# Moving a gather from behind the wait for a scattering addition to ahead of it, in a kernel of graph layers and experts

## The chip, the cores and the metric

One core of one Trainium2 chip runs the whole program. The metric is device microseconds of one execution; the time before is the median of three timed runs. The core has five engines with their own instruction streams: TensorE (PE), VectorE (DVE), ScalarE (ACT), GpSimd (POOL) and SyncE (SP). They meet at semaphores only. DMAs are issued from POOL's, SP's and ACT's streams and run on 16 DMA engines; each adds 16 to a semaphore when it has landed.

## The reference

3125 nodes with 256 features go through four blocks, each added to its input: a graph network of three layers with batch norm, an attention over 64 slices, a second graph convolution of two layers, and a mixture of experts. Only the last one is touched:

```
logits = xt @ Wr + br;  probs = softmax(logits)
top_p, top_idx = top_k(probs, 2);  weights = top_p / top_p.sum()
xn = (xt - mean) * rsqrt(var + 1e-5)
xe = xn * ln_g[e] + ln_b[e]                      # for each of 8 experts
h  = gelu(xe @ W1[e] + b1[e])                    # 256 -> 1024
y  = h @ W2[e] + b2[e]                           # 1024 -> 256
out = x + sum over the two chosen experts of weight * y
```

## The kernel before

The graph blocks come first and end at about 2550 us. Then the router picks two experts for each node. The kernel computes only chosen pairs of node and expert: it sorts them by expert into units of 128 rows, and units into 32 chunks (CHUNKS) of one expert each. Each chunk has two units, but every fourth has one (UNITS_OF, L53): a turn (TURN = 4) has 2, 2, 2 and 1 units, 56 in all. The loops of the engines run over eight turns g of four chunks j; chunk c = 4g + j uses buffer s = c % 2 of everything that is double: the gathered rows xin, the expert's weights w1e and w2e, the outputs yrow, the banks of PSUM.

One chunk c passes through these steps, named by their lines:

- POOL gathers its rows from the DRAM table xn_rows into xin[c % 2], one indirect DMA for each unit (gather_rows, L616 to L621). Its index table, from_row, comes from the router (r_dve reaches 3). Before the buffer is written again, TensorE must have read chunk c - 2 from it: e_tps counts the transposed chunks.
- SP loads W1 of the chunk's expert and its vectors (load_rows, L483 to L488) when ScalarE is done with chunk c - 2, and W2 and b2 (load_second, L490 to L493) when VectorE is done with the outputs of chunk c - 2 (e_y).
- TensorE turns the rows (turn_rows, L2069), waiting for row_in, the gather's semaphore; VectorE applies the expert's norm vectors (L1615); TensorE computes the hidden layer (hidden, L2079: 32 matmuls), ScalarE its GELU (L902), and TensorE the outputs (outputs, L2088: 16 matmuls for each unit, as 32 instructions in the profile for two).
- VectorE adds b2 (L1623) and multiplies by the gate (L1625) into yrow[c % 2], and adds one to e_y. It waits for y_used at c + 1, that is, until the additions of chunk c - 2 have landed.
- POOL adds the rows to x_sum in DRAM, one indirect DMA with addition for each unit (L642). A node can stand in two chunks, and two additions to one row must not be in flight together, so POOL waits for all of a chunk's additions to land (y_added, L644) before it issues those of the next; then it adds one to y_used (L645).

TensorE's order is fixed: transposes of chunk c + 1, outputs of chunk c, hidden layer of chunk c + 1 (turn_of_chunks, L2095 to L2104). POOL's order is the loop at L635 to L645. Before the loop POOL gathers chunks 0 and 1 (L631, L632) and waits until x_sum is stored (moe_stored) and the index table of the additions is there (r_dve reaches 4). In the loop, iteration c first gathers chunk c + 2 and then adds chunk c. After the last chunk SP and ACT wait for y_used and copy x_sum to the output.

Of the kernel before, what the change touches and what calls it, by code (L numbers as in the profile page):

```python
# [43 lines left out]
CHUNKS = PAIRS + SINGLES  # L44
# [51 lines left out]
def build(nc, x, src, dst, w, out):  # L96
    ctx = ExitStack()
    with ctx:
# [219 lines left out]
        def fresh(tag, *names):  # L318
            return [sem(f"{tag}_{n}") for n in names]
# [25 lines left out]
        e_tps, e_xe, e_hps, e_gelu, e_yps, e_b, e_y = fresh("expert", "transposed", "inputs", "hidden", "gelus", "outputs", "biased", "rows_out")  # L345
# [168 lines left out]
        def _(pool):  # L514
# [101 lines left out]
            def gather_rows(c):  # L616

                for i in range(UNITS_OF[c]):
                    j = UNIT_AT[c] + i
                    nc.gpsimd.indirect_dma_start(out=xin[c % 2][:, i, :], out_offset=None, in_=xn_rows,  # L620
                                                 in_offset=bass.IndirectOffsetOnAxis(ap=from_row[:, j:j + 1], axis=0)).then_inc(row_in[c % 2], 16)  # L621
# [8 lines left out]
            pool.wait_ge(r_dve, 3)  # L630
            gather_rows(0)  # L631
            gather_rows(1)  # L632
            pool.wait_ge(moe_stored, 16 * 5)
            pool.wait_ge(r_dve, 4)
            for c in range(CHUNKS):  # L635
                if c + 2 < CHUNKS:
                    pool.wait_ge(e_tps, c + 1)
                    gather_rows(c + 2)
                pool.wait_ge(e_y, c + 3)
                for i in range(UNITS_OF[c]):  # L640
                    j = UNIT_AT[c] + i
                    nc.gpsimd.indirect_dma_start(out=x_sum, out_offset=bass.IndirectOffsetOnAxis(ap=to_row[:, j:j + 1], axis=0),  # L642
                                                 in_=yrow[c % 2][:, i, :], in_offset=None, compute_op=ALU.add).then_inc(y_added, 16)
                pool.wait_ge(y_added, 16 * sum(UNITS_OF[:c + 1]))  # L644
                pool.sem_inc(y_used, 1)  # L645

# [2 lines left out]
        def _(act):  # L649
# [195 lines left out]
            def conv_rows(k):  # L845

                _, tps, tcp, xps, hi, _ = conv

                def copy(t, i):
                    wait(tps, t + (k * T + BT + 1))  # L850
                    nc.scalar.activation(feat[:, 0:2, i * P:(i + 1) * P], ps[:, i % 2, 0:F].rearrange("p (f c) -> p f c", f=2), ACT.Copy).then_inc(tcp, 1)

                def high(t, i):
                    wait(xps, t + (k * T + 1))
                    nc.scalar.activation(conv_halves[0][0][:, bass.ds(t, 1), 0:F], ps[:, 2 + i % 2, 0:F].unsqueeze(1), ACT.Copy, scale=sc[:, 0:1]).then_inc(hi, 1)

                if k == 0:
                    block_sqrt(0)
                    wait(sc_ready, 3)
                    for t in range(T + 1):  # L860
                        if t < T:
                            copy(t, t % BT)
                        if t >= 1:
                            high(t - 1, (t - 1) % BT)
                        if t % BT == 2 and t // BT + 1 < NB:
                            block_sqrt(t // BT + 1)
                else:
                    wait(sc_ready, 4)
                    three_stages(act.Fori(1, NB), copy, high, nothing)
# [772 lines left out]
        def _(pe):  # L1642
# [54 lines left out]
            def enter_block(l, b, tile_rows, weights, last=HB):  # L1697

                rows, _, lo = ent[l][0:3]
                for h, tiles in ((0, (0, 1)), (1, (2, 3, 4))):  # L1700
                    for i in tiles:
                        pe.wait_ge(lo, b * BT + (2 if i == 4 else 1))
                        for f in range(4):
                            if i == tiles[0]:
                                pe.wait_ge(rows, b * 8 + (4 * h + f + 1))
                            ins = tile_rows(i, f)
                        ins.then_inc(ent[l][3], 1)
                    half_products(l, b, h, weights, HB if h == 0 else last)
# [253 lines left out]
            def conv_rows(k):  # L1962

                rows, tps, tcp, xps, _, lo = conv

                def turn(t, i):
# [166 lines left out]
```

## Time and profile before

| | |
|---|---|
| timed runs | 3054.23 us median (3053.55 to 3055.42, three runs) |
| the profiled execution's own time | 3055.43 us |
| its span, first to last instruction | 3053.6 us |
| mean granted TensorE clock | 0.868 of full speed |
| TensorE busy | 2275.3 us, 75% of the span |
| POOL busy | 888.4 us, 29%, of which the gathers and additions of the expert chunks are a small part |
| first gather of the stage, last addition issued | 2592.7 us, 3037.1 us |

The profile is one execution, recorded by the hardware. Line numbers (L620) are those of the kernel's code. A row of the timeline gives start, busy time, engine, line, operation, what is written and read, how many instructions are merged, and in brackets how long the engine was idle before and who ended that. harena and ring are large buffers in SBUF in which xin, xeT, yrow and the experts' weights lie under their own names: in this stage a POOL row that writes harena from xn_rows is a gather, and ring is W1 and W2. "issue" is time in which nothing that the profile shows was waited for.

### The profile page before, as it was taken

The numbers are of one execution on the slowest core, as the hardware profiler recorded it, in microseconds if no ns is written. First come the engines' busy times: TensorE is split into PE (matmuls) and PEld (weight loads), VectorE is DVE, ScalarE is ACT, GpSimd is POOL, SyncE is SP. The second block draws the span as 40 slices with busy tenths as digits, with TensorE's granted clock in tenths as the row PEclk, the third lists the DMA queues.
The fourth block names the chain that finished last, engine by engine and source line by source line (L and its number), as shares of the span: only waits on it lengthen the run. The fifth ranks groups of instructions, "written<-read, shape, count | busy, mean of one in ns | idle before, by whom it ended". The sixth has DMA issues, their size and how long they took to land.

```text
span 3053.6 us, 39654 instructions
## 1 busy us (share of the span) xinstructions
PE 2275.3 (75%) x14187; PEld 1775.8 (58%) x14187; DVE 1314.2 (43%) x2799; ACT 375.8 (12%) x789; POOL 888.4 (29%) x638
## 2 busy tenths in 40 slices
PE   1033100069779999999988977999899995999997
PEld 1022100046557776778763456888688884788886
DVE  7899999954431111111127743113311667111111
ACT  0011000000015000004002202000210000222221
POOL 4888888878800000000011300000100001233332
PEclk6566555579989999999998969999999996999998
DMA  9943333398550999950460000444234434566665
GB/s 338 339 67 48 42 55 48 35 310 249 137 192 0 181 260 218 261 172 0 137 192 0 0 1 11 150 145 148 83 119 150 138 103 128 162 194 208 185 191 170
DMA packets 287137, 425.19 MB, mean 139 GB/s; under 512 B 165698, under 2 KB 222553, under 8 KB 286975
## 3 DMA queue, kind: packets, MB, share of 16 engines
q1 hardware_dynamic: 104895, 295.72, 29.9%
q10 hardware_dynamic: 109760, 108.33, 13.1%
q0 software_dynamic: 72400, 20.04, 7.8%
q8 instruction: 51, 0.84, 0.1%
q14 instruction: 31, 0.25, 0.0%
HBM read 306.57 MB, written 100.17 MB: 133 GB/s over the span
## 4 chain that ended last, share of the span: by engine, by line
PE 59%; POOL 16%; DVE 10%; issue 7%; DMA 5%; ACT 2%; DVEq 0%; ACTq 0%; SPq 0%; POOLq 0%
PE ps L1762 16%; PE ps L2008 8%; PE ps L2009 8%; POOL at_counts L552 8%; POOL odd_counts L552 7%; PE ps L2088 6%; PE ps L1780 4%; PE ps L1694 4%; PE ps L2079 4%; DMA x_sum<-harena 2%; PE ps L1951 2%; PE ps L1848 2%; DMA xrows<-odd_counts 1%; PE ps L1977 1%; DMA harena<-xn_rows,harena 1%
## 5 line engine op out<-in xcount | busy, mean ns | idle before, releaser
L2008 PE MATMUL ps<-harena,ring 128*128 128x257 f16 x2500 | 556.7, 275 | 3.7 <-DVE harena L1361 2.7
L2009 PE MATMUL ps<-harena,ring 128*128 128x256 f16 x2500 | 556.4, 274 | 0.0
L1762 PE MATMUL ps<-ring,harena 128*128 128x320 f16 (+1 forms) x4000 | 539.2, 297 | 1.4 <-ACT tarena L713 0.8
L1762 PEld LDWEIGHTS ps<-ring,harena 128*128 128x128 f16 x4000 | 391.9, 98 | 144.6 <-issue 3.1
L1056 DVE SCALAR_TENSOR_TENSOR late<-ring,ps 128x1024 f16<-128x1024 f32 x312 | 378.9, 1275 | 12.3 <-DMA ring<-key_rows 10.1
L552 POOL DMA_INDIRECT at_counts<-harena x208 | 330.7, 1590 | 110.0 <-issue 104.0
L552 POOL DMA_INDIRECT odd_counts<-harena x208 | 328.7, 1580 | 63.7 <-issue 61.8
L2008 PEld LDWEIGHTS ps<-harena,ring 128*128 128x128 f16 x2500 | 243.7, 97 | 43.2 <-DVE harena L1427 3.8
L2009 PEld LDWEIGHTS ps<-harena,ring 128*128 128x128 f16 x2500 | 243.2, 97 | 33.0
L1786 PE MATMUL ps<-ident,sc 128*1 128x128 f32 x8 | 2.1, 365 | 288.5 <-DVE sc L1004 288.5
L2088 PE MATMUL ps<-ring,harena 128*128 128x256 f32 x896 | 202.2, 384 | 7.8 <-ACT harena L902 6.6
L2079 PE MATMUL ps<-harena,ring 128*128 128x256 f32 (+1 forms) x1024 | 202.5, 357 | 1.2 <-DVE harena L1615 1.2
L2079 PEld LDWEIGHTS ps<-harena,ring 128*128 128x128 f32 x1024 | 178.0, 193 | 22.2 <-issue 1.6
L2088 PEld LDWEIGHTS ps<-ring,harena 128*128 128x128 f32 x896 | 169.0, 191 | 34.9 <-issue 13.5
L1137 DVE SCALAR_TENSOR_TENSOR feat<-ps,sc,late 128x640 f32<-128x640 f32 x30 | 26.5, 883 | 348.5 <-PE ps L1762 348.5
L577 POOL DMA_DIRECT2D wl<-L_ffn_W_out x1 | 0.7, 712 | 586.8 <-DVE feat L1137 586.8
L1786 PEld LDWEIGHTS ps<-ident,sc 128*1 128x1 f32 x8 | 0.4, 81 | 290.2 <-issue 284.0
L902 ACT ACTIVATE harena<-ps,harena 128x256 f32<-128x256 f32 (+1 forms) x256 | 114.4, 447 | 358.6 <-PE ps L2079 354.2
L1371 DVE TENSOR_SCALAR late<-ps 128x1 f32<-128x1 f32 x100 | 15.4, 154 | 325.0 <-PE ps L2009 325.0
L1780 PE MATMUL ps<-feat,wl 128*128 128x320 f32 x480 | 134.8, 442 | 18.3 <-DVE feat L1137 17.2
L609 POOL COPY feat<-tarena 128x256 f32 x25 | 9.8, 400 | 438.0 <-DVE tarena L1432 414.3
L642 POOL DMA_INDIRECT x_sum<-harena x56 | 89.1, 1590 | 145.1 <-DVE harena L1625 135.7
(382 smaller groups left out, 2620.1 us busy)
## 6 DMA issues: line engine op xcount, KB each, us to landing
ring<-at_counts SPq DMA_DIRECT2D x150, 800.0 KB, 4.5
ring<-L_ffn_W SPq DMA_DIRECT2D x64, 1024.0 KB, 5.5
ring<-ad_counts SPq DMA_DIRECT2D x50, 800.0 KB, 4.2
ring<-key_rows SPq DMA_DIRECT2D x52, 512.0 KB, 3.8
at_counts<-tarena ACTq DMA_DIRECT2D x5, 4000.0 KB, 15.0
odd_counts<-tarena ACTq DMA_DIRECT2D x5, 4000.0 KB, 27.2
xrows<-odd_counts SPq DMA_DIRECT2D x25, 800.0 KB, 8.3
at_counts<-ring ACTq DMA_DIRECT2D x25, 800.0 KB, 7.5
```

The costliest lines, as they stand in the source:

```text
L552: nc.gpsimd.indirect_dma_start(out=table, out_offset=bass.IndirectOffsetOnAxis(ap=eidx[:, c:c + 1], axis=0), in_=evalue[:, c:c + 1], in_of ...
L642: nc.gpsimd.indirect_dma_start(out=x_sum, out_offset=bass.IndirectOffsetOnAxis(ap=to_row[:, j:j + 1], axis=0), in_=yrow[c % 2][:, i, :], i ...
L902: nc.scalar.activation(hT[s][:, k, 0:n], ps[:, k % 4, 0:n], ACT.Gelu, bias=evc[s][:, k:k + 1]).then_inc(e_gelu, 1)
L1056: ins = V.scalar_tensor_tensor(out=ejunk[q], in0=krow[:, s, :], scalar=ekey[:, bass.ds(g + q, 1)], in1=weight_ps[:, GE - P - q * P:2 * GE ...
L1694: ins = M(ps[:, 4 + n % 4, 0:c], weights[:, d, fo * P:(fo + 1) * P], feat[:, d, h * HB:h * HB + c], start=(d == 0), stop=(d == 3))
L1762: ins = M(ps[:, 2 * f + h, 0:c], part[:, t, (2 * k + f) * P:(2 * k + f + 1) * P], chunk[q][:, s, h * HB:h * HB + c], start=(t == 0 and par ...
L1780: ins = M(ps[:, k + h, 0:HB], wl2[:, d, fo * P:(fo + 1) * P], feat[:, d, h * HB:(h + 1) * HB], start=(d == 0), stop=(d == nfi - 1))
L1848: return M(ps[:, i % 4, 0:F], feat[:, d, i * P:(i + 1) * P], wl3[:, d, :], start=(d == 0), stop=(d == 3))
L2008: M(ps[:, i, 0:F + 1], lhs, hh[:, t, 0:F + 1], start=(t == 0), stop=False)
L2009: ins = M(ps[:, i, 0:F], lhs, hl[:, t, :], start=False, stop=(t == T - 1))
L2079: ins = M(ps[:, k % 4, 0:n * P], w1e[s][:, d, k * P:(k + 1) * P], xeT[s][:, d, 0:n * P], start=(d == 0), stop=(d == 1))
L2088: ins = M(ps[:, 4 + s, i * F:(i + 1) * F], hT[s][:, k, i * P:(i + 1) * P], w2e[s][:, k, :], start=(k == 0), stop=(k == EK - 1))
```

## The change

POOL's loop gathers three chunks ahead instead of two, and at another place: after the additions of chunk c are issued and before the wait for their landing. Chunk 2 is gathered ahead of the loop. A gather of chunk c + 3 writes buffer (c + 3) % 2 = (c + 1) % 2, so it waits for the transposes of chunk c + 1 (e_tps at c + 2). All other engines' streams are the same.

```diff
             gather_rows(0)
             gather_rows(1)
+            pool.wait_ge(e_tps, 1)
+            gather_rows(2)
             pool.wait_ge(moe_stored, 16 * 5)
             pool.wait_ge(r_dve, 4)
             for c in range(CHUNKS):
-                if c + 2 < CHUNKS:
-                    pool.wait_ge(e_tps, c + 1)
-                    gather_rows(c + 2)
                 pool.wait_ge(e_y, c + 3)
                 for i in range(UNITS_OF[c]):
                     j = UNIT_AT[c] + i
                     nc.gpsimd.indirect_dma_start(out=x_sum, out_offset=bass.IndirectOffsetOnAxis(ap=to_row[:, j:j + 1], axis=0),
                                                  in_=yrow[c % 2][:, i, :], in_offset=None, compute_op=ALU.add).then_inc(y_added, 16)
+                if c + 3 < CHUNKS:
+                    pool.wait_ge(e_tps, c + 2)
+                    gather_rows(c + 3)
                 pool.wait_ge(y_added, 16 * sum(UNITS_OF[:c + 1]))
                 pool.sem_inc(y_used, 1)
```

## Rows read from the trace of the kernel before

**Rows 1.** The page, part 4: the chain that ended last, by line.

```profile
PE ps L1762 16%; PE ps L2008 8%; PE ps L2009 8%; POOL at_counts L552 8%; POOL odd_counts L552 7%; PE ps L2088 6%; PE ps L1780 4%; PE ps L1694 4%; PE ps L2079 4%; DMA x_sum<-harena 2%; PE ps L1951 2%; PE ps L1848 2%; DMA xrows<-odd_counts 1%; PE ps L1977 1%; DMA harena<-xn_rows,harena 1%
```

**Rows 2.** Waits, 2590 to 3053 us: who for whom, total us, times, longest.

```profile
DVE harena L1623 <- PE ps L2088: 180.9, 32, 7.0
...
POOL harena L620 <- DMA x_sum<-harena: 130.5, 25, 7.8
...
PE ps L2069 <- DMA harena<-xn_rows,harena: 21.8, 8, 5.1
```

**Rows 3.** Timeline of PE: a boundary without a wait, two with one.

```profile
2616.79 7.07 PE L2079 MATMUL ps<-harena,ring 128*128 128x256 f32 x32
2623.70 0.60 PE L2069 MATMUL ps<-ident,harena 128*128 128x128 f32 x4
2624.56 7.17 PE L2088 MATMUL ps<-ring,harena 128*128 128x256 f32 x32 [0.26 <-ACT harena L902]
...
2654.23 7.07 PE L2079 MATMUL ps<-harena,ring 128*128 128x256 f32 x32
2663.80 0.66 PE L2069 MATMUL ps<-ident,harena 128*128 128x128 f32 x4 [2.50 <-DMA harena<-xn_rows,harena]
2664.29 7.07 PE L2088 MATMUL ps<-ring,harena 128*128 128x256 f32 x32
...
2708.63 7.07 PE L2079 MATMUL ps<-harena,ring 128*128 128x256 f32 x32
```

**Rows 4.** The chain in order of time: start us, us, what.

```profile
2650.28 8.55 DMA x_sum<-harena
...
2660.99 2.77 DMA harena<-xn_rows,harena
...
2704.68 6.27 DMA x_sum<-harena
...
2713.11 5.25 DMA harena<-xn_rows,harena
...
2923.61 8.25 DMA x_sum<-harena
```

**Rows 5.** Timeline of POOL: gathers (L620), additions (L642).

```profile
2598.75 0.94 POOL L620 DMA_INDIRECT harena<-xn_rows,harena  x1 [1.15 <-PE ps L2069]
...
2650.28 1.59 POOL L642 DMA_INDIRECT x_sum<-harena  x1 [0.31 <-issue]
2659.67 1.01 POOL L620 DMA_INDIRECT harena<-xn_rows,harena  x1 [7.81 <-DMA x_sum<-harena]
```

**Rows 6.** Landings: additions L642; gathers L620; the gather issued at 2711.8.

```profile
DMA to landing us min/median/max: 3.7/6.4/8.6
...
DMA to landing us min/median/max: 2.7/3.5/5.2
...
DMA to landing us min/median/max: 4.7/4.7/4.7
```

**Rows 7.** Two us: engines' busy time; last PEclk, DMA share, GB/s.

```profile
2656.00:2658.00 2.00, 2.00 (x11) 1.77 (x10) 0.00 (x0) 1.00 (x3) 0.00 (x0) 1.00 1.07 345
```

**Rows 8.** W1 issued at 2651.4, its landing; all W2 (L492); VectorE's timeline.

```profile
L486 SPq DMA_DIRECT2D ring<-L_ffn_W x1: 378/378/378, 2651.4 to 2651.4; - x1
...
DMA to landing us min/median/max: 7.9/7.9/7.9
...
DMA to landing us min/median/max: 5.2/5.6/10.4
...
2671.49 0.69 DVE L1623 TENSOR_TENSOR harena<-ps,harena 128x512 f32<-128x512 f32 x1 [5.90 <-PE ps L2088]
```

**Rows 9.** PE's timeline in turn 4, and five us of it (last PEclk, DMA share, GB/s).

```profile
2826.89 1.12 PE L2069 MATMUL ps<-ident,harena 128*128 128x128 f32 x4 [2.31 <-DMA harena<-xn_rows,harena]
2827.80 8.22 PE L2088 MATMUL ps<-ring,harena 128*128 128x256 f32 x32
...
2825.00:2830.00 5.00, 3.11 (x10) 2.67 (x11) 0.99 (x2) 0.14 (x1) 1.50 (x2) 0.67 0.79 219
```

## The prediction

> **What bounds the kernel now.** I read the page's chain first [rows 1]: matmul lines fill it; the additions into x_sum landing are 2% of the chain, the gathers landing 1%. The change lies in the last stage alone, the 32 expert chunks from 2592 us on, so everything ahead of it stays. The second view, the waits of that stage [rows 2], says who is late there. TensorE's transposes (L2069) wait for gathered rows 8 times, 21.8 us together. VectorE's L1623 waits for TensorE in all of its 32 turns, never for additions to land. POOL waits 130.5 us for landings: long, and costly only where it holds back a gather that TensorE wants.
>
> The third view, TensorE's own order of time, says where [rows 3]. At a boundary without a wait (2616.79) the transposes come 6.91 us behind the start of the hidden layer L2079, and the outputs L2088 7.77 us behind it. The boundary at 2654.23 has the same instructions, but 2.50 us of idle before the transposes. It is the same place in each turn of four chunks (of two, two, two and one unit): the transposes of chunk 4g+5. There are seven, g = 0 to 6. The eighth wait is the first gather of the stage, 5.10 us from 2591.7 to 2596.83, which the change leaves alone. So the seven make 21.8 - 5.1 = 16.7 us.
>
> The chain of that stretch and POOL's order show why there [rows 4, 5]. The second addition of chunk 2 is issued at 2650.28 and lands after 8.55 us, at 2658.8; POOL wakes, issues the gathers of chunk 5 at 2659.67 and 2660.99, and the latter lands 2.77 us on, at 2663.8. TensorE could have used the rows from 2654.23 + 6.91 = 2661.14. Chunk 3 has one unit and so half the matmuls of the others: this interval is some 7 us shorter (half of 7.07 + 7.17) [rows 3] than those that hide the same sequence.
>
> **The change, part by part.** Nothing is added or removed: 56 gathers and 56 additions before and after, the same waits on the same semaphores. Three things move.
>
> The gather of chunk 2 moves ahead of two waits, for stores and for indices. It still waits for the first transposes, and its issue at 2598.75 came 1.15 us behind its forerunner and right behind them [rows 5], so the two waits cost nothing there: 0 us.
>
> The gathers of chunk c+3 move from behind the landing of chunk c's additions to ahead of it. For chunk 5, POOL issues them at 2650.28 + 1.59 + 0.30 = 2652.2 and, 1.01 and 0.30 later, at 2653.5: 7.5 us earlier than before. Their own wait, for chunk c+1's transposes, never holds: TensorE runs those before outputs(c), and outputs(c) comes before the additions. How long do they take to land? Gathers of the stage take 2.7 to 5.2 us, median 3.5 [rows 6]; the long one was issued at 2713.11 [rows 4] into full DMA engines, and they are as full here (share 1.07 in 2656 to 2658) [rows 7]. So I take the upper end: 2653.5 + 5.2 = 2658.7, 2.4 us before TensorE wants them, and the stall goes whole. With 2.7 us they land at 2656.2, which brings no more. No gather of this trace was issued with an addition still in flight ahead of it; that bound is under rival A.
>
> The step "landed, count up" (y_used) moves past two gathers, 2 x 1.3 = 2.6 us of POOL. The shortest landing is 3.7 us [rows 6], 1.6 of it the issue itself, so the step is late by 0.5 us at most. VectorE asks for it at L1623 two chunks on: for chunk 2's additions, landed at 2658.8, at 2671.49 [rows 8]. Some 12 us of cover, 10 after the change: 0 us. POOL's next additions come earlier, as the gathers no longer stand before them.
>
> SP's queue is not passed, only its DMA engines shared: two units (128 rows of 256 fp32 each, 0.26 MB) now travel while the weights do, of which W1 alone has 1 MB. W1 of chunk 5, issued at 2651.4, lands in 7.9 us, at 2659.3, and is wanted by the next hidden layer, at 2669 after the change; W2 of chunk 4, issued with chunk 2's additions, is wanted at 2661.9, over 13 us on, and the longest landing of any W2 is 10.4 us [rows 8]. A quarter megabyte against the load that took 7.9 us is 2 us at most, less than either cover (9.7 and 3.3): 0 us. What is late next at the boundary is ScalarE's last GELU, 0.26 us as at 2624.56 [rows 3].
>
> **The sum.** L2079 to L2088 takes 2664.29 - 2654.23 = 10.06 us with the stall and 7.77 without: 2.29 us. The outputs behind a stall are busy 7.07 us, elsewhere 7.17 [rows 3], so 0.1 goes back. That is 2.2 us for 2.5 us of idle: 0.3 less, because transposes that come late hide behind nothing. Over seven, 16.7 - 7 x 0.3 = 14.6 us. Turn 4 has more: after 2.31 us of idle the granted clock was 0.67 in 2825 to 2830 (of the levels 2.4 and 1.2 GHz, the lower for two thirds of that time), the transposes took 1.12 instead of 0.66 us and the outputs 8.22 instead of 7.07 [rows 9]. That is 1.6 us, which goes too if the idle was what let the clock fall; six equal stalls did not make it fall, so it may not be in each execution. Against the profiled one (span 3053.6, time 3055.43): 16.2 us, so 3039.2. The median of the runs, 3054.23, lies 1.2 below that one, about this clock event; less 14.6 it gives 3039.6. I predict 3039.5.
>
> **A rule beside the rows.** The row: chunk 2's second addition lands 8.55 us after its issue, at 2658.8 [rows 4]. The Trainium skill's "DMA: Bandwidth & Descriptors" says, in "Queues, rings and completion order", that a DMA engine takes the descriptors of one ring in order, and that a semaphore's increment lands only after every earlier write of that engine, whatever the queue. By that rule the gathers, in POOL's queue behind the additions, cannot be counted in before 2658.8, however early they are issued. No row of this trace has a gather behind an addition in flight.
>
> **Rivals.**
> *A. The gathers queue behind the additions.* They then land one unit at a time after the last addition. Under load the two gathers of turn 2 landed 1.9 us apart (2711.80 + 4.7 and 2713.11 + 5.25) [rows 4, 6]; at best both come in with the addition. So 0 to 3.8 us after it. From addition to need there are 2661.14 - 2658.83 = 2.3 us in turn 1, and 2715.54 - 2710.95 = 4.6 in turn 2; three turns have additions like the first (8.55 to 8.25 us) [rows 4]. These three keep 0 to 1.5 us of wait each, 0 to 4.5 us in all; with 2.5 us, 3042.0. For it: one queue. Against it: the additions' 8 us may be a wait for the weights' loads that the gathers share and need not repeat.
>
> *B. The stall is DMA volume, not order.* TensorE restarts 9.57 us after L2079's start in turn 1 and 9.77 in turn 2 (2718.4), although the additions took 8.55 and 6.27 us; the gathers made up for it with 2.77 and 5.25 [rows 3, 4]. That looks like rows that come in when the weights' backlog clears, whatever POOL does. If they then land at 2662.8 instead of 2663.8, the gain is 7 x 1 us: 3047. Against it: W1 of chunk 5, four times the two units and issued 2 us ahead of their new place, was in at 2659.3 [rows 8].
>
> *C. Slower: gathers and additions in one queue hold each other up.* The additions read and write x_sum in DRAM, the gathers read beside them. If a gather issued at 2653.5 takes over 10.3 us (to 2663.8, where TensorE starts today), each boundary is later than now; at 12 us, 1.7 x 7 = 12 us more, 3066. It decides from twice the longest gather of the trace. For it only that the pair is never seen in flight together; against it that two additions together still land in 8.6 us.
>
> *D. Order isn't what holds the gathers.* If POOL could not issue a gather before the additions ahead of it are done, the time stays at 3054. Against it: the second addition is issued 0.31 us behind the first [rows 5], with that in flight.
>
> **Chances.** Forecast (stall gone, 3037 to 3041) 0.60; A 0.23; B 0.09; C 0.04; D 0.04. The range, 3036.5 to 3046.5, holds the forecast with and without the clock event, A to its worst bound and part of B. A measurement here tells about 0.2% (6.1 us) from no change. Faster by more: forecast, A and two thirds of B, 0.89. Within: the rest of B, and D, 0.07. Slower: C, 0.04.
>
> **What would show it.** In the changed kernel's waits of the stage, L2069 should have one wait for gathered rows (5.1 us) and at most a few under 1 us; L2079 to L2088 7.8 us in all turns; a turn of 52 us, not 54.4 (2654.23 to 2708.63). POOL's gathers stand 0.3 us behind additions. The landing of the boundary gathers tells the forecast from A: 3 to 5.2 us, or behind the addition each time. B shows as landings at the same distance from L2079 as now, C as landings above 10 us. I am wrong if TensorE gets a new wait, on weights or on y_used by way of VectorE, or if those gathers take over 7.6 us.

## The result, and the profile after

The changed kernel takes 3039.19 us (median of five runs, 3039.01 to 3042.78), the one before 3055.42 (3053.55 to 3065.41). The ratio is 0.9945, 95% interval 0.9925 to 0.9964: faster by 0.55%, well clear of 0.2%. The forecast was 3039.5; the five runs after the change alone spread over 3.8 us, so part of that closeness is luck. The profiled executions have spans of 3037.4 and 3053.6 us, 16.2 apart, which is the sum that the prediction made against the profiled execution.

Two lines stand above the loop now, so other lines have shifted: L2071 are the transposes (L2069 before), L2081 the hidden layer (L2079), L2090 the outputs (L2088), L1625 VectorE's first step on them (L1623), L641 the additions (L642); the gathers stay L620.

The waits of the expert stage, who for whom, total us, times, longest:

```profile
POOL x_sum L641 <- DVE harena L1627: 233.9, 25, 17.9
DVE harena L1625 <- PE ps L2090: 183.3, 32, 6.9
...
POOL x_sum L641 <- DMA x_sum<-harena: 25.7, 7, 5.4
...
PE ps L2071 <- DMA harena<-xn_rows,harena: 5.3, 1, 5.3
```

Of the eight waits for gathered rows one is left, the first of the stage; before it was 21.8 us in eight [rows 2]. VectorE still waits for TensorE alone, 32 times. POOL waits for landings only seven times, ahead of the additions of the one-unit chunks; the rest of its time it now waits for outputs, as it should.

TensorE's order of time, at a boundary that had no wait and at two that had one:

```profile
2616.97 7.07 PE L2081 MATMUL ps<-harena,ring 128*128 128x256 f32 x32
2623.88 0.60 PE L2071 MATMUL ps<-ident,harena 128*128 128x128 f32 x4
2624.74 7.17 PE L2090 MATMUL ps<-ring,harena 128*128 128x256 f32 x32 [0.26 <-ACT harena L904]
...
2654.41 7.07 PE L2081 MATMUL ps<-harena,ring 128*128 128x256 f32 x32
2661.32 0.60 PE L2071 MATMUL ps<-ident,harena 128*128 128x128 f32 x4
2662.18 7.17 PE L2090 MATMUL ps<-ring,harena 128*128 128x256 f32 x32 [0.27 <-ACT harena L904]
...
2706.62 7.07 PE L2081 MATMUL ps<-harena,ring 128*128 128x256 f32 x32
```

L2081 to L2090 is 7.77 us at both, where it was 10.06 at the second [rows 3]; a turn is 2706.62 - 2654.41 = 52.21 us, where it was 54.40. The granted clock shows it too, in five us of turn 4 (the last three numbers are granted clock, DMA share, GB/s): 1.00 with TensorE at work, where 2825 to 2830 had 0.67 [rows 9].

```profile
2815.00:2820.00 5.00, 4.73 (x25) 3.96 (x24) 0.99 (x2) 2.13 (x5) 2.74 (x3) 1.00 1.04 303
```

POOL's order at the boundary, and two landings, of the addition issued at 2650.45 and of the gather issued at 2653.67:

```profile
2650.45 1.59 POOL L641 DMA_INDIRECT x_sum<-harena  x1 [0.30 <-issue]
2652.35 1.01 POOL L620 DMA_INDIRECT harena<-xn_rows,harena  x1 [0.30 <-issue]
2653.67 0.99 POOL L620 DMA_INDIRECT harena<-xn_rows,harena  x1 [0.30 <-issue]
2657.19 1.61 POOL L641 DMA_INDIRECT x_sum<-harena  x1 [2.53 <-DMA x_sum<-harena]
```

```profile
DMA to landing us min/median/max: 5.9/5.9/5.9
...
DMA to landing us min/median/max: 6.2/6.2/6.2
```

The gather takes 6.2 us, not 2.77 as before or 5.2 as forecast, and lands at 2659.87, 3.5 us behind the addition and 1.45 us ahead of the transposes. The seven boundaries, in us from the issue of the second addition (before: landing of the addition, then TensorE's restart on the rows; after: the same landing, the second gather's landing and TensorE's transposes, which did not wait):

| turn | before: addition, restart | after: addition, gather, transposes |
|---|---|---|
| 1 | 8.55, 13.52 | 5.9, 9.4, 10.87 |
| 2 | 6.27, 13.72 | 6.4, 9.2, 10.86 |
| 3 | 6.70, 13.38 | 7.0, 9.5, 10.85 |
| 4 | 6.25, 13.33 | 8.7, 9.7, 10.85 |
| 5 | 8.31, 13.39 | 7.9, 9.7, 10.85 |
| 6 | 8.25, 13.23 | 6.8, 9.4, 10.85 |
| 7 | 7.32, 13.29 | 6.5, 9.5, 10.85 |

In both kernels the rows come at nearly the same point of each turn, while the addition's landing moves by 2.3 to 2.8 us. That does not look like a queue in which the addition alone sets when a gather lands; it is what the experiments had to settle.

**Where the time went.** I measure the stage by the distance between two transposes that the first gather doesn't touch, those of chunk 1 and of chunk 31: 3020.05 - 2608.92 = 411.13 us before, 3004.03 - 2609.10 = 394.93 after. The difference is 16.20 us, all of the 16.2 of the spans; what lies outside moved by 0.2 us each way. This distance repeats to some 0.02 us (394.92 or 394.93 in each kernel below that has no stall), whereas whole executions of one kernel differ by several us, mostly from stages before this one (the first transposes came at 2595.6 to 2625.0 us in the profiles of this study). So below the times tell gain or no gain, and the distance and the waits tell the sizes.

### The profile page after: what moved, and what is told of

Same layout as the page of the kernel before. It is cut to its first block, busy times and chain, and to the rows that moved or that the text cites. A ratio compares the mean times of both kernels' runs of the same rounds, so it can differ in the third digit from the quotient of the medians.

```text
span 3037.4 us, 39654 instructions
## 1 busy us (share of the span) xinstructions
PE 2268.6 (75%) x14187; PEld 1770.3 (58%) x14187; DVE 1314.5 (43%) x2799; ACT 375.7 (12%) x789; POOL 890.2 (29%) x638
## 4 chain that ended last, share of the span: by engine, by line
PE 61%; DVE 20%; issue 8%; DMA 4%; ACT 2%; ACTq 2%; DVEq 1%; POOL 0%; SPq 0%
PE ps L1764 16%; PE ps L2010 8%; PE ps L2011 8%; PE ps L2090 7%; PE ps L2081 6%; DVE late L1058 6%; PE ps L1782 4%; PE ps L1696 4%; DVE ring L1058 3%; DMA odd_counts<-tarena 3%; PE ps L1953 2%; PE ps L1850 1%; DMA xrows<-odd_counts 1%; ACTq L672 1%; PE ps L1979 1%
## 5 line engine op out<-in xcount | busy, mean ns | idle before, releaser
L2090 PE MATMUL ps<-ring,harena 128*128 128x256 f32 x896 | 201.7, 382 | 9.7 <-ACT harena L904 8.2
L2081 PE MATMUL ps<-harena,ring 128*128 128x256 f32 (+1 forms) x1024 | 201.2, 355 | 1.2 <-DVE harena L1617 1.2
L2090 PEld LDWEIGHTS ps<-ring,harena 128*128 128x128 f32 x896 | 167.6, 190 | 38.5 <-issue 17.0
L2081 PEld LDWEIGHTS ps<-harena,ring 128*128 128x128 f32 x1024 | 176.8, 192 | 22.2 <-issue 1.6
L641 POOL DMA_INDIRECT x_sum<-harena x56 | 89.0, 1590 | 266.9 <-DVE harena L1627 233.9
```

The source lines that it names most:

```text
L2081: ins = M(ps[:, k % 4, 0:n * P], w1e[s][:, d, k * P:(k + 1) * P], xeT[s][:, d, 0:n * P], start=(d == 0), stop=(d == 1))
L2090: ins = M(ps[:, 4 + s, i * F:(i + 1) * F], hT[s][:, k, i * P:(i + 1) * P], w2e[s][:, k, :], start=(k == 0), stop=(k == EK - 1))
```

## The experiments

**Is it the seven boundaries, and the place rather than the depth?** Two kernels.

```diff
 # e1: the kernel before, with
-                if c + 2 < CHUNKS:
+                if c + 2 < CHUNKS and c % TURN != TURN - 1:
                     pool.wait_ge(e_tps, c + 1)
                     gather_rows(c + 2)
 ...
+                if c + 3 < CHUNKS and c % TURN == TURN - 2:
+                    pool.wait_ge(e_tps, c + 2)
+                    gather_rows(c + 3)
                 pool.wait_ge(y_added, 16 * sum(UNITS_OF[:c + 1]))
```

> The kernel before, with one gather of each turn moved: that of chunk 4g+5 is issued behind chunk 4g+2's additions and ahead of the wait for their landing; all others stay two chunks ahead. My theory (seven stalls at one place in the turn, each 2.2 to 2.5 us, and nothing else) expects the whole gain of the change: 3039 us, L2069 with one wait for gathered rows. The rival, that the other 24 chunks' earlier gathers take load off the DMA engines at the boundary and so have a share in it, expects a part of the stalls back: 3042 or more.

Measured: 3039.76 us against 3055.16 (ratio 0.9928, 0.9902 to 0.9954), distance 394.93 us. TensorE's transposes (L2072 here) wait once, for the first gather of the stage:

```profile
PE ps L2072 <- DMA harena<-xn_rows,harena: 5.3, 1, 5.3
```

The whole gain comes from seven of the 30 moved gathers (a chunk's gathers counted as one).

```diff
 # e2: the changed kernel, with
+                pool.wait_ge(y_added, 16 * sum(UNITS_OF[:c + 1]))
                 if c + 3 < CHUNKS:
                     pool.wait_ge(e_tps, c + 2)
                     gather_rows(c + 3)
-                pool.wait_ge(y_added, 16 * sum(UNITS_OF[:c + 1]))
```

> The changed kernel with the gather still three chunks ahead, but behind the wait for the additions' landing (and ahead of y_used). My theory, that the place ahead of the landing is all of the gain and the depth of the look-ahead nothing, expects the time of before, 3054 to 3055 us, and 16 to 17 us of waits at L2069 in seven boundaries. The rival, that looking further ahead is what helps, expects 3039 to 3045.

Measured: 3055.15 against 3055.16 (ratio 1.0006, 0.9971 to 1.0041); distance 409.56. The waits at the seven boundaries are 18.5 - 5.1 = 13.4 us, less than the 16 to 17 expected. POOL's order there, and TensorE's waits of the stage:

```profile
2651.01 1.59 POOL L641 DMA_INDIRECT x_sum<-harena  x1 [0.30 <-issue]
2659.77 1.01 POOL L620 DMA_INDIRECT harena<-xn_rows,harena  x1 [7.17 <-DMA x_sum<-harena]
```

```profile
PE ps L2071 <- DMA harena<-xn_rows,harena: 18.5, 8, 5.1
```

Looking further ahead buys next to nothing by itself: the gathers come out behind the landing, where they stood in the kernel before. What is left of a gain, some 0.5 us in each turn, has a likely reason that no run isolates: POOL issues the first gather 0.3 us behind the landing (2651.01 + 8.5) and counts y_used up afterwards, where the kernel before counts first and issues 0.8 us behind it (2658.83, 2659.67).

**How much room is left, and what fills it?** Two kernels put a fill of an idle buffer between the boundary's additions and gathers.

```diff
 # e7: 2260 columns; e8: 4520
+                if c % TURN == TURN - 2:
+                    o.mark(nc.gpsimd.memset(tarena[:, 0:2260], 0.0))
+                    o.settle()
                 if c + 3 < CHUNKS:
```

> The changed kernel with the boundary gathers (chunks 4g+5) held back about 2.2 us: POOL fills 2260 columns of an idle buffer between the additions and the gathers. The second gather then goes out near 2655.9 of the changed kernel's trace; it landed at 2659.9, 1.45 us ahead of the need (1.15 to 1.66 in the seven turns). If its landing moves along with its issue, 0.5 to 1 us of wait in each turn, 3043 to 3046. If landings are bound to the additions ahead of them or to the load's end, they stay where they are or move by 1 us: 3039 to 3041.

> The same with 4520 columns, about 4.2 us: the second gather goes out near 2658, still 3 us ahead of the kernel before. If the landing moves along with the issue: 2.5 to 3 us of wait in each turn, all of the gain gone, 3056. If a gather is faster the later it goes (4 to 5 us here, as the load thins out): it lands at 2662 to 2663, 1 to 1.5 us of wait each, 3047 to 3050.

Measured for e7: 3040.11 against 3055.37 (ratio 0.994, 0.9918 to 0.9963), distance 395.97. The second gather goes out 5.2 us behind the second addition, 2.0 us later than in the changed kernel. Five of the seven boundaries wait 0.27 to 0.72 us, the other two 0.1 us or less; this is 1.0 us of distance, not the 4 to 7 that I wrote.

```profile
PE ps L2074 <- DMA harena<-xn_rows,harena: 7.8, 6, 5.3
```

The time falls into the range that I gave for a landing that stays where it is, yet the landing did move with the issue: from the issue to TensorE's start on the rows it is 5.8 to 6.6 us, and the room, 1.1 to 1.6 us in the changed kernel, took most of the 2.0.

Measured for e8: 3055.53 against 3055.37 (ratio 1.0011, 0.9981 to 1.0041), distance 407.68. All the gain in time is gone and 12.75 of the 16.20 us of distance, against my 7 to 11 for a gather that gets faster. The waits of 1.74 to 2.02 us lie between my two forecasts (2.5 to 3, and 1 to 1.5). POOL's and TensorE's rows at the first boundary:

```profile
2647.96 1.59 POOL L641 DMA_INDIRECT x_sum<-harena  x1 [0.31 <-issue]
...
2653.70 1.02 POOL L620 DMA_INDIRECT harena<-xn_rows,harena  x1 [0.27 <-POOL tarena L644]
2655.02 0.99 POOL L620 DMA_INDIRECT harena<-xn_rows,harena  x1 [0.30 <-issue]
```

```profile
2660.91 0.66 PE L2074 MATMUL ps<-ident,harena 128*128 128x128 f32 x4 [1.93 <-DMA harena<-xn_rows,harena]
```

The second gather goes out 7.1 us behind the second addition, 3.6 us sooner than in the kernel before (10.7), and the rows come at 12.95 instead of 13.52: 3.6 us earlier in issue bought 0.6 us. Something other than POOL sets the end there. SP's rows in the changed kernel show what lies in between:

```profile
2648.42 0.37 SPq L492 DMA_DIRECT2D ring<-L_ffn_W  x1
...
2651.98 0.38 SPq L486 DMA_DIRECT2D ring<-L_ffn_W  x1
...
2655.73 0.37 SPq L492 DMA_DIRECT2D ring<-L_ffn_W  x1
```

These are three loads of 1 MB: W2 of chunk 4, W1 of chunk 5, W2 of chunk 5. The third goes out 5.3 us behind the second addition. The changed kernel's gathers (3.2) are ahead of it; e7's (5.2) are level with it; those of e8, e2 and the kernel before behind.

**Is it the load?** First all of it: an eighth of W1 and W2 for chunks 2 to 31, in the changed kernel (e4) and in the kernel before (e5). Both compute with stale weights. The edit in words:

```diff
+    w1e[s][:, :, 0:P]  <- W1[e, :, 0:P]      # instead of all 1024 columns
+    w2e[s][:, 0:1, :]  <- W2[e, 0:P, :]      # instead of all 8 blocks of rows
```

> The changed kernel with an eighth of W1 and W2 loaded for chunks 2 to 31 (128 of 1024 hidden columns, one of eight row blocks); the matmuls run as before on what lies in the buffers. It shows what sets the 6 us that boundary gathers take. If it is the weights' load beside them: additions land in 3.8 to 4.8 us, gathers in 2.7 to 3.9, as where no load is beside them. If it is only the place behind the additions in POOL's queue, the gathers stay above 5 us. The time stays at 3039 by both.

> The kernel before, its order untouched, with an eighth of W1 and W2 loaded for chunks 2 to 31. POOL's serial chain at the boundary is landing of the additions, 0.8 us to wake, 1.3 us to issue, landing of the gather. If the weights' load is what makes it too long: 2650.3 + 4.5 + 0.8 + 1.3 + 2.8 = 2659.7, ahead of the need at 2661.1, the stalls go without any change of order, and the time is 3039. If order alone makes the stall, it stays near 3054.

e4 took 3038.0 us in its one run, distance 394.92, no wait at a boundary. Its trace holds no landing times of gathers; what it was to show can be read from the packets of POOL's queue, further down, together with e6. e5 took 3039.66 against 3055.37 (ratio 0.9936, 0.9909 to 0.9962), distance 394.92. The order is that of the kernel before, and the seven stalls are gone. Landings of its additions (L642), and the transposes' waits:

```profile
DMA to landing us min/median/max: 3.7/4.2/4.4
```

```profile
PE ps L2069 <- DMA harena<-xn_rows,harena: 5.2, 1, 5.2
```

Additions land in 4.2 us at the median instead of 6.4 [rows 6]. So the stall has two conditions, POOL's serial order and the megabytes beside it; taking either away is enough (the changed kernel, e5).

Then load by load, in the kernel before, an eighth of one matrix for every second chunk.

```diff
 # e9:  load_second(e, s, 1 if s == 1 else EK)          -> W2 of chunk 4g+5
 # e10: load_rows(g * 2 + s, s, P if s == 1 else EH)    -> W1 of chunk 4g+5
 # e12: load_second(e, s, 1 if s == 0 else EK)          -> W2 of chunk 4g+4
```

> The kernel before with an eighth of W2 loaded for odd chunks from 3 on, the others whole: at the boundary this takes away the load of W2 for chunk 4g+5, which goes out 5.3 us behind the second addition, ahead of the gathers' issue. Theory after the first eight runs: a gather issued behind that load lands with its end, some 13 us behind the second addition, whatever its issue. Then rows should now come 1.5 to 2 us earlier: stalls of 0.3 to 1 us, 3044 to 3047. If the load does not matter, 2.2 to 2.7 us each and 3054.

> The kernel before with an eighth of W1 loaded for odd chunks from 3 on: at the boundary this takes away the load that goes out 1.2 us behind the second addition and lies beside its landing. If the additions' long landing (6.3 to 8.6 us) is time shared with that load, they land in 4 to 5.5 us, POOL issues the gathers 2 to 3 us earlier, yet behind the load of W2 for chunk 4g+5: stalls of 0.5 to 1.5 us, 3045 to 3050. If any megabyte counts alike, the same as the run with less W2.

> The kernel before with an eighth of W2 loaded for even chunks: at the boundary this takes away the load for chunk 4g+4, which goes out together with the additions and lands before their wait is over; the two loads that follow stay. It is the control for the other two: if a gather lands with the end of W2 of chunk 4g+5, most of the stall stays, 1.5 to 2.3 us each, 3049 to 3053; if any megabyte counts alike, as those.

| | time, us | ratio (95%) | distance | mean wait | gather's issue ahead of need | issue to restart |
|---|---|---|---|---|---|---|
| before | | | 411.13 | 2.39 | 1.48 | 3.87 |
| e9 | 3047.98 | 0.9987 (0.9963 to 1.0011) | 401.13 | 0.96 | 1.85 | 2.81 |
| e10 | 3043.21 | 0.9960 (0.9947 to 0.9973) | 399.15 | 0.90 | 3.12 | 4.02 |
| e12 | 3049.01 | 0.9990 (0.9974 to 1.0006) | 399.91 | 1.01 | 3.30 | 4.31 |

The last three columns are means over the seven boundaries, for the second gather, in us; "ahead of need" is issue to restart less the wait. The kernel before ran at 3054.08 beside them. The waits of e9 and e12 are shorter for sure (11.9 - 5.2 = 6.7 and 12.2 - 5.2 = 7.0 us instead of 16.7), but their times are not told apart from before. Two times miss their forecasts: e9's 3047.98 lies above 3044 to 3047, with one turn of 2.27 us of wait among waits of 0.35 to 1.23, and e10's 3043.21 below 3045 to 3050. The three rows of waits, e9, e10, e12:

```profile
PE ps L2069 <- DMA harena<-xn_rows,harena: 11.9, 8, 5.2
```

```profile
PE ps L2069 <- DMA harena<-xn_rows,harena: 11.5, 8, 5.2
```

```profile
PE ps L2069 <- DMA harena<-xn_rows,harena: 12.2, 8, 5.2
```

The theory that W2 of chunk 4g+5 alone holds the gathers predicted 1.5 to 2.3 us for e12; it was 0.86 to 1.53, and above 1.10 in one turn only. It falls in that form: each of the three megabytes is worth the same, 1.4 to 1.5 us of wait. How each works differs. Without W2 of chunk 4g+5 the gather itself is quick (2.74 to 2.86 us at each boundary) and what remains is the addition's landing, issue by issue. Without one of the earlier two, the additions land sooner, the gathers go out 1.6 to 1.8 us earlier, and then take 4.0 to 4.3 us beside the last load.

**Is it the additions, ahead in POOL's queue?**

```diff
 # e6: the changed kernel, no additions at the boundary, a fill in their place
+                if c % TURN == TURN - 2:
+                    o.mark(nc.gpsimd.memset(tarena[:, 0:3900], 0.0))
+                    o.settle()
-                for i in range(UNITS_OF[c]):
+                for i in range(UNITS_OF[c] if c % TURN != TURN - 2 else 0):
 ...                # and y_added is awaited without the additions left out
 # e11: the same in e8, whose gathers come too late by 1.9 us
```

> The changed kernel without the additions of chunks 4g+2; in their place POOL fills 3900 columns of an idle buffer, about 3.5 us, so that the boundary gathers are issued at the time they were. If the gathers wait behind the additions in POOL's queue (rival A of the prediction), they now land in 3 to 4.5 us instead of 6.0 to 6.8. If only the weights' load beside them counts, they stay at 5.5 or more. The time stays at 3039.

> The kernel with the boundary gathers 4 us later (1.7 to 2.0 us of wait in each turn) without the additions of chunks 4g+2, POOL filling 3900 columns in their place, so that the gathers go out at the same time. If gathers land late because they stand behind additions in POOL's queue, the waits now fall under 0.5 us: 3040 to 3042. If it is the weights' load ahead of them, 1.3 to 2 us each stay: 3049 to 3056.

The time of e6 tells nothing (its one run took 3057.59 us with a distance of 394.93; its stage began 17 us late), neither kernel has a wait to read it from, and its trace holds no landing times of gathers. But e6 and e4 hold every packet of POOL's queue (q0). The two additions and the two gathers of a boundary are 384 packets with 0.52 MB, the two gathers alone 96 with 0.26 MB. Three stretches of the first turn follow (packets, MB, share of the engines' time): the changed kernel from the issue of the first addition to 5.5 us behind the issue of the second gather (2648.54 to 2659.17); e4 likewise, but to 3.0 us behind it (2647.45 to 2655.58); e6 from the issue of the first gather to 4.0 us behind that of the second (2670.28 to 2675.53):

```profile
q0 software_dynamic: 384, 0.52, 22.1%
```

```profile
q0 software_dynamic: 384, 0.52, 38.8%
```

```profile
q0 software_dynamic: 96, 0.26, 12.8%
```

Over the seven turns the last of these packets starts 5.5 to 6.1 us behind the second gather's issue in the changed kernel, 2.3 to 2.7 in e4 and 4.0 to 4.5 in e6; in the changed kernel the landing follows 0.4 to 0.8 us later. So e4 came out as I had written for the load: behind two additions in flight, but without the megabytes, the gathers are as quick as those of e9, which go out behind landed additions and 7 us or more behind the last whole megabyte (2.3 to 2.5 us to the last packet). In e6 the landing, reckoned the same way, is 4.4 to 5.3 us, between my two ranges and nearer to that of the queue. With the megabytes there, the additions ahead cost the gathers some 1.5 us at the changed kernel's place; that is an estimate, as e6's gathers also went out 0.5 us further ahead of the need.

e11 is the same question where there is a wait: 3045.64 against 3054.08 (ratio 0.9969, 0.9959 to 0.9979), distance 399.23, mean wait 0.91 us where e8 had 1.88.

```profile
PE ps L2077 <- DMA harena<-xn_rows,harena: 11.6, 8, 5.2
```

Its gathers went out 4.36 us ahead of the need, e8's 3.96. If landings move along with the issue, that is 0.40 of the 0.97, and the additions' part is 0.57 us: issue to restart is 5.27 us without them and 5.84 with them. If they do not, it is up to 0.97. Both of my ranges missed it. At this later place the additions ahead in the queue cost a gather half a microsecond to one, the loads beside it about two and a half (5.27 against 2.81 in e9, which still had the two earlier ones).

**Can the room be made larger?** e3 puts the gather ahead of the additions.

```diff
             for c in range(CHUNKS):
+                if c + 3 < CHUNKS:
+                    pool.wait_ge(e_tps, c + 2)
+                    gather_rows(c + 3)
                 pool.wait_ge(e_y, c + 3)
 ...
-                if c + 3 < CHUNKS:
-                    pool.wait_ge(e_tps, c + 2)
-                    gather_rows(c + 3)
```

> The changed kernel with the gather of chunk c+3 moved once more, ahead of the wait for chunk c's outputs and so ahead of its additions, right behind the transposes that free its buffer. My theory expects 3039 us again, since no stall is left to take away, and the boundary gathers landing 3 to 5 us after an issue near 2642, which is 15 us ahead of the need instead of 1.2 to 1.7 us. The rival, that TensorE is still held back by DMA traffic at the boundary, expects up to 2 us less.

```profile
2642.15 1.01 POOL L620 DMA_INDIRECT harena<-xn_rows,harena  x1 [4.55 <-DMA x_sum<-harena]
2643.47 0.97 POOL L620 DMA_INDIRECT harena<-xn_rows,harena  x1 [0.31 <-issue]
2648.86 1.62 POOL L644 DMA_INDIRECT x_sum<-harena  x1 [4.41 <-DVE harena L1627]
```

Measured: 3038.28 against 3055.16 (ratio 0.9925, 0.9898 to 0.9952), distance 394.92: the same as the changed kernel, no stall at either. TensorE is not held by DMA at the boundary in any other way. The wait of 4.55 us in the first row is that for chunk 1's additions, behind which these gathers now stand. They go out at 2643.5, 18.2 us ahead of the transposes at 2661.6, where the changed kernel has 7.65 and needs 6.0 to 6.5 of it (the second gather's landings). Their last packets start 2.5 to 3.2 us behind the issue, before the first of the three loads goes out. It is the version I would keep. It does not beat the changed kernel by anything that these runs can tell.

## Why the prediction was right

**The place and the size of the stalls: right.** Seven boundaries, and nothing else of the change, hold the gain (e1). The sum of 14.6 us and 1.6 us for the clock is 16.2, and the distance shrank by 16.20. (The forecast of 3039.5 goes by the smaller sum and a median before of 3054.23, which came out as 3055.42 over five runs.) Each part of the sum shows: 10.06 to 7.77 us, and 7.17 instead of 7.07 us of outputs given back.

**The clock event: right in size, open in its frequency.** It shows as a step of 15.9 to 16.0 instead of 14.3 us from the transposes of a boundary to the next ones. It came at 5 of the 23 boundaries that waited 1.5 us or more (one in the kernel before, two in e2, one each in e8 and e9, after waits of 1.93 to 2.32 us), at none of the 31 that waited less and at none of those without a wait. So a stall costs 2.2 us and now and then 1.6 more.

**Zero for what moved: right.** No wait of VectorE for y_used, none of TensorE for weights. The loads beside the gathers did get slower, within their cover: over the seven turns the third load of the boundary took 6.6 to 6.9 us instead of 5.9 to 6.2, and W1 7.7 to 8.4 instead of 7.3 to 7.9.

**The gather's landing: wrong, and without effect on the time.** I took 5.2 us, the longest of the trace, as the upper end; at the boundary gathers took 6.0 to 6.8, and the room left was 1.1 to 1.6 us instead of 2.4. No gather of the trace before had additions in flight ahead of it, and together with the loads these cost 1.5 us (e6). By the test that the prediction named, 3 to 5.2 us or behind the addition each time, rival A's landings came, and the forecast's time held because they still left room. This is the one step that could have cost the gain: e8 is the changed kernel with 4 us less of room, and has none left.

**Rival A** had the order right, as the rule of the Trainium skill's "DMA: Bandwidth & Descriptors" ("Queues, rings and completion order") would have it: at the boundaries the gathers landed 0 to 3.5 us behind the addition ahead of them, within the 0 to 3.8 given. But order alone does not decide. In turn 4 the addition landed at 8.7 and the gather at 9.7, in turn 1 at 5.9 and 9.4; taking the additions away brings the gathers' last packets 1.5 us forward (e6), taking the loads away 3 us (e4). The waits of up to 1.5 us that A gave three turns did not come. **Rival B**, volume, is one of the two conditions of the stall (e5, e9, e10, e12), and yet wrong as a forecast: what it left out is that a gather issued ahead of the last load is not held by it. From 10.7 to 7.1 us the issue bought 0.6; from 7.1 to 5.2 and 3.2 it bought 1.2 and 3.5. **Rival C**: additions and gathers in flight together land in 5.9 to 8.7 and 6.0 to 6.8 us, no trace of its 10. **Rival D** is refuted by POOL's rows: gathers are issued 0.30 us behind additions in flight.

## What to carry to other kernels

When an in-order engine both feeds and drains a pipeline, issue the feed before you wait for the drain, and look for the one interval that is shorter than the rest: only there was the wait on the path. Read a transfer's latency with what will be in flight at its new place, ahead of it in its own queue and beside it: here it rose from 3.8 us to 6.3 in the mean of the seven second gathers, and the gain stood on 1.1 to 1.6 us of room. Where a buffer is free long before, issue the prefetch there (e3) rather than just ahead of the wait; it cost nothing that these runs can tell, and the rows were in before the loads went out.

## What the hardware showed unexpectedly

A gather of 128 rows of 1 KB took 2.8 us from issue to use where no load of a megabyte was issued in the 7 us ahead of it (e9) and 5.8 behind two of them and two additions (e8), though it moves an eighth of one load; without the additions it was 5.3 (e11). Two additions in flight ahead of the gathers cost them at most 0.3 us where the loads were small (e4 against e9) and some 1.5 us where they were whole (e6), so order in the queue and volume beside it do not simply add up. Three loads of a megabyte each had the same price at the boundary, 1.4 to 1.5 us, whether they went out together with the additions, behind them, or between additions and gathers. I did not try whether smaller pieces of the loads would let a gather through sooner.
